# A state-space block: a third state weighed by TensorE, and the second chunk's first in-projection in front of unit 0

## The reference

```python
xz = (hidden_states @ in_proj_w.T).transpose(0, 2, 1)
x, z = jnp.split(xz, 2, axis=1)
# each direction: a convolution of 4 taps over time, a projection to dt, B and C, and then per channel d and state n
def step(h, inp):
    u_t, dt_t, B_t, C_t = inp
    dA = jnp.exp(dt_t[:, :, None] * A)
    h = dA * h + (dt_t * u_t)[:, :, None] * B_t[:, None, :]
    y = jnp.einsum('bdn,bn->bd', h, C_t)
    return (h, y)
y = (y_fwd + y_bwd) * jax.nn.silu(z.transpose(0, 2, 1))
out = y @ out_proj_w.T
```

## Time and profile before

| | us |
|---|---|
| median of 3 runs (lowest, highest) | 8235.12 (8234.53, 8238.75) |
| the profiled execution, its own time | 8231.93 |
| its span in the trace | 8230.1 |
| busy: VectorE, TensorE (matmul), GpSimd, ScalarE | 7156.1, 7136.7, 6715.8, 5349.8 |
| first scan of unit 0 starts at | 728.41 |
| last work of VectorE on unit 255 ends at | about 7181 |

### The profile page before, as it was taken

One profiled execution on the slowest core, in us unless ns is written; L12 is line 12 of the kernel. 1 busy time (PEld: TensorE's weight loads), 2 busy tenths in 40 slices (PEclk: granted clock), 3 DMA queues, 4 the chain that ended last, 5 costly groups with the idle time before them and its releaser, 6 DMA issues. The chain is left out here.

```text
span 8230.1 us, 114768 instructions
## 1 busy us (share of the span) xinstructions
PE 7136.7 (87%) x32512; PEld 4393.1 (53%) x32512; DVE 7156.1 (87%) x7788; ACT 5349.8 (65%) x12640; POOL 6715.8 (82%) x2320
## 2 busy tenths in 40 slices
PE   6578888888888888877899999999999988789999
PEld 3344555555555555554555555555555555534444
DVE  6913999999999999999999999999999999934443
ACT  6634777777777777777777777777777777610000
POOL 5513999999999999999999999999999999821110
PEclk8789999999999999998999999999999999889999
DMA  3363232323232323221323232323233332153442
GB/s 103 90 191 128 70 118 66 118 70 118 67 118 68 119 67 118 68 98 44 113 79 128 76 128 77 131 79 126 89 116 104 104 107 70 63 191 133 136 140 76
DMA packets 557719, 844.05 MB, mean 103 GB/s; under 512 B 129472, under 2 KB 276928, under 8 KB 539712
## 3 DMA queue, kind: packets, MB, share of 16 engines
q1 hardware_dynamic: 557120, 837.10, 31.1%
HBM read 583.89 MB, written 253.02 MB: 102 GB/s over the span
## 5 line engine op out<-in xcount | busy, mean ns | idle before, releaser
L1192 POOL TENSOR_TENSOR scan_w<-scan_du,scan_bcast_b 128x2048 f32<-128x2048 f32 x1023 | 4623.9, 4544 | 45.0 <-DVE scan_h L1239 6.6
L1239 DVE TENSOR_TENSOR_SCAN scan_h<-scan_da,scan_state,scan_w 128x512 f32<-128x512 f32 x2560 | 3185.3, 1276 | 44.2 <-ACT scan_da L1094 27.7
L1094 ACT ACTIVATE scan_da<-scan_delta,scan_prm 128x512 f32<-128x512 f32 x4096 | 2803.1, 685 | 0.0
L973 PE MATMUL scan_yT<-all_ident,scan_hc 128*128 128x128 f32 x10240 | 1540.1, 281 | 660.4 <-DVE scan_hc L1249 659.6
L1239 DVE TENSOR_TENSOR_SCAN scan_hs<-scan_da,scan_state,scan_w 128x512 f32<-128x512 f32 x1536 | 1891.9, 1258 | 45.2 <-ACT scan_da L1094 44.7
L973 PEld LDWEIGHTS scan_yT<-all_ident,scan_hc 128*128 128x128 f32 x10240 | 1175.3, 143 | 1395.5 <-DVE scan_hc L1249 1047.1
L846 PE MATMUL scan_in_ps<-scan_hn,scan_win 128*128 128x512 f32 x3840 | 1732.3, 594 | 13.6 <-issue 13.6
L1249 DVE TENSOR_TENSOR scan_hc<-scan_h,scan_bcast_c 128x512 f32<-128x512 f32 x2560 | 1637.3, 671 | 2.1 <-ACT scan_state L1074 0.7
L1202 POOL TENSOR_TENSOR scan_hp<-scan_hs,scan_bcast_c 128x1024 f32<-128x1024 f32 x512 | 1209.3, 2362 | 49.9 <-DVE scan_hs L1239 42.9
L846 PEld LDWEIGHTS scan_in_ps<-scan_hn,scan_win 128*128 128x128 f32 x3840 | 693.6, 191 | 715.6 <-issue 715.6
L1074 ACT ACTIVATE scan_state<-scan_h 128x1 f32<-128x1 f32 x2560 | 429.5, 168 | 982.8 <-DVE scan_h L1239 977.0
(11 more groups left out here) (122 smaller groups left out, 6918.3 us busy)
## 6 DMA issues: line engine op xcount, KB each, us to landing
yT<-scan_y_out SPq DMA_DIRECT2D x257, 256.0 KB, 2.0
scan_win<-winx SPq DMA_DIRECT2D x128, 512.0 KB, 3.7
xc<-scan_xc_out SPq DMA_DIRECT2D x256, 256.0 KB, 2.0
scan_xc<-xc SPq DMA_DIRECT2D x256, 256.0 KB, 4.1
scan_bcast_b<-bc SPq DMA_DIRECT2D x64, 1024.0 KB, 8.0
scan_bcast_c<-bc SPq DMA_DIRECT2D x64, 1024.0 KB, 8.2
scan_win<-winz SPq DMA_DIRECT2D x128, 512.0 KB, 4.6
scan_x<-x_pad SPq DMA_DIRECT2D x128, 257.5 KB, 2.6
```

What stands on the lines that cost most here:

```text
L973: last = nc.tensor.matmul(yT[:, tb], hc_slot(b, n)[:, tb * P:(tb + 1) * P], ident[:], is_transpose=True, start=(i == 0 and tb == 0), stop= ...
L1094: nc.scalar.activation(da[:, n % 2], delta[:, s], ACT.Exp, scale=decay(b, n)).then_inc(S["exp_done"], 1)
L1192: nc.gpsimd.tensor_tensor(w[:, g], du[:].unsqueeze(1).to_broadcast([P, G, T]), bcast_b[:, g * G:(g + 1) * G], ALU.mult).then_inc(S["w_done ...
L1239: nc.vector.tensor_tensor_scan(flip(b, h_slot(b, n)), flip(b, da[:, n % 2]), flip(b, w[:, n // G, n % G]), state_of(b, n), ALU.mult, ALU.a ...
```

## The change

1. State 1 moves from VN to TN: nine states are weighed by VectorE, three by TensorE (1, 4 and 10). `c_col`, `c_diag` and `hs` grow by one entry each; `y_out` shrinks from two buffers to one, so that `yT_copy(b)` waits until the stores of unit b itself have landed, where it waited for those of unit b - 1.
2. The new state is turned in `dt_ps`, the convolution's bank, in TensorE's step 3, copied in ScalarE's step 7 ahead of the copy out of `in_ps`, and added in TensorE's step 7. The convolution (step 5) now waits for that copy.
3. `C_DIAG_AT` has twelve entries and begins in step 2 (it had eight and began in step 3). `TURN`, the table of units 111 to 127, is gone: they use `NORMAL`.
4. The in-projection of unit 16's x (a = DB) and its copy stand in front of unit 0; the next one (`LATER`) moves to unit 0's steps 0, 2 and 7. SyncE's loads of `hn` and of two blocks of `win` for them move ahead of the last two blocks of `before_scan`.

```diff
-TN = [4, 10]
+TN = [1, 4, 10]
...
-        y_out = sc.sb("y_out", [P, 2, TB, P])
+        y_out = sc.sb("y_out", [P, TB, P])
...
-        EARLY = dict(into=(0, 2), diag=1, copy=5, conv=5, xc=8, proj=8)
-        TURN = dict(diag=1, conv=2, xc=7, proj=8)
-        LATER = dict(into=(8, 10), diag=6, copy=11, conv=11, xc=12, proj=13)
+        EARLY = dict(into=(), diag=1, copy=NS, conv=5, xc=8, proj=8)
+        LATER = dict(into=(0, 2), diag=6, copy=7, conv=9, xc=12, proj=13)
...
-            return [(a, TURN if back(b) and not back(a) else NORMAL)] if a < NU else []
+            return [(a, NORMAL)] if a < NU else []
...
-            if b == 0:
-                return dict(mm=(6, 12), copy=(10, NS - 1), add=(12, NS - 1))
-            return dict(mm=(8, 12), copy=(12, NS - 1), add=(12, NS - 1))
+            return dict(mm=(3, 8, 12), copy=(7, 12, NS - 1), add=(7, 12, NS - 1))
+
+        def turn_bank(k):
+            return in_ps if k else dt_ps
...
-        C_DIAG_AT = (3, 3, 8, 8, 9, 9, 11, 11)
+        C_DIAG_AT = (2, 2, 3, 3, 8, 8, 9, 9, 11, 11, 13, 13)
...
-                for a in range(2):
-                    load_win(DB + a)
...
-                load_hn(1)
...
+                if j == DB // 2 - 1:
+                    hold(sp, S["in_mm"], DB, S["passed"])
+                    load_win(DB)
+                    load_hn(1)
+                    load_win(DB + 1)
...
+                if k == 0:
+                    pe.wait_ge(S["dt_read"], min(b + 2, NU))
+                    pe.wait_ge(S["xc_copied"], min(b + DB + 1, NU) + 2 if b else DB + 2)
...
             def conv_step(a, b):
                 pe.wait_ge(S["dt_read"], min(b + 2, NU))
+                pe.wait_ge(S["h_turn_copied"], b * NTN + 1)
...
             dt_matmul(0)
+            in_step(DB, 0, 0)
+            in_step(DB, 1, 0)
...
-                if b >= 1:
-                    act.wait_ge(S["stored"], stored_to(b - 1))
+                if b >= 0:
+                    act.wait_ge(S["stored"], stored_to(b))
...
+                    if n == turn_steps(b)["copy"][0]:
+                        turn_copy(b, 0)
...
+            act.wait_ge(a_in[DB % 2], (DB // 2 + 1) * (NA * LOAD))
+            in_copy(DB)
             for b in range(NU):
                 unit(b)
```

19 lines of the change are left out of this document (10 added, 9 removed).

## The result

The changed kernel takes 8206.67 us (median of 12 runs, 8201.99 to 8219.13); the kernel before, run beside it, 8234.45 (12 runs, 8222.72 to 8238.75). The ratio is 0.9971 with a 95% interval of 0.9963 to 0.9978: 28 us won. The forecast was 8205, its range 8165 to 8245. The total is right. Of the parts that make it up one has the wrong sign, and another, which was given nothing, cost 5 us. The span of the profiled execution is 8201.3 us.

What follows compares the result with a forecast made beforehand. It took GpSimd's unchanged pitch of 24.86 us as a floor under every unit, beside VectorE's equal pitch. Front -13, steady backward -4, forward -2, units 112 to 127 -8 sum to -27: 8205 us, range 8165 to 8245.

Steps and rivals of the forecast that it cites:

- The front: Up to unit 1: ScalarE's waits for the first two in-projections go; -13 us (-20 to +2).
- Steady backward units: Units 16 to 111: between GpSimd's floor of 2386.6 and VectorE's own 2396 us; -4 us (0 to -9).
- the forecast floor: GpSimd's unchanged pitch of 24.86 us under every unit; 96 x 24.86 = 2386.6 us for units 16 to 111.
- VectorE's own pitch becomes 24.75: Steady units: 24.84 less 0.59 for the removed weighing, plus 0.50 for ScalarE's added copy stalling scan 8.
- TensorE stays off the path as long as its clock holds: Every unit: TensorE gains 0.89 us, 23.2 us a unit backward and 23.7 forward, below 24.84 both times.
- VectorE alone is the bound: Rival: GpSimd's equal pitch is an echo; 152 us over 256 units and 13 at the front, 8067 us; chance 0.05.
- Forward units: Units 128 to 239: clock lapses go, chunk ends cost VectorE 6.2 us each; -2 us (-25 to +40).
- The lapses of the clock: Units 128 to 239: TensorE's clock halves after idle time in one unit of three; worth 21 us, should go.
- The rival's price: Rival of slower chunk ends: 6 us more at each of seven forward ends, 42 us, 8247 us; chance 0.12.
- Units 112 to 127: Units without in-projection, 415.3 us before: -8 us, from -17 at best to +5 if both stalls stay and grow.
- It takes a wait out of ScalarE's tight chain: Units 112 to 127: convolution from step 2 to 5, its copy from 7 to 10; part of the -8 us.
- Chunk ends: Forward ends: columns and y copy wanted sooner, 3 us each, with copy (0.5) and two diagonals (0.6) 4.1 more.

Runs made afterwards that it cites:

- the front alone: Kernel before plus only the early first in-projection, its loads and copy in front of unit 0, two turned states and two y buffers kept: 8217.73 us, ratio 0.9985.
- the filler: Changed kernel plus TensorE matmuls whose result nobody reads, two groups in units 111 to 127 and one in units 240 to 255: 8175.64 us, ratio 0.9926.

## Why the prediction came out, and where it didn't

*The total*: 8205 forecast, 8206.67 measured. -13, -4, -8, -2 and 0 met -16 (with -3 in the rest of chunk 0), -8, +10, -10 and +5, and -6 from a stretch in which nothing changed. Some of that is luck.

*The front*: right in mechanism, -16 for -13. I had put 4 us on hn's load going ahead of the last stores and the first scan at 737; it started at 732.96 in the profiled run. In other kernels with the same front it started at 731 to 748 us, so single executions differ here by as much as the term itself. Alone it was worth 14 us.

*Steady backward units*: 2387.3, within 0.7 us of the forecast floor of 2386.6, yet not because of the floor. The step that failed is the sentence that VectorE may be shortened and GpSimd's unit is still the pitch. With GpSimd 1.1 us a unit lighter nothing moved. "VectorE's own pitch becomes 24.75" was 24.70, with 0.35 of stall where I had 0.5; that the scan which stalls is scan 8, behind ScalarE's copy, is as in the trace. By the prediction's own sum VectorE needed 2396, and -4 was a choice between that and the floor; the 0.05 us a unit and six chunk ends at 2.7 us each, where I had 3.4, are the whole distance to 2387.3. That the result lies on the floor is luck. What I had not seen is the second way to the same scan: "TensorE stays off the path as long as its clock holds" was argued from its busy time, 23.2 of 24.84 us. In the changed kernel the turn in step 3 hangs behind 9.7 us of TensorE's work, and that ring closes in 24.68 us. The rival "VectorE alone is the bound" (8067) is refuted too: the stall in front of scan 8 doesn't go with GpSimd.

*Forward units*: -10.4 for -2, inside its range, by two sizes. The lapses of the clock went, as forecast (granted clock 1.00), and chunk ends cost VectorE 2807.1 - 112 x 24.70 = 40.7 us, 5.8 each, where I had 6.2. The pitch made the rest: 24.70 and not 24.75 gives 5.6 us. But the seven are not alike. Chunk 8 begins behind a backward end and takes 397.9, 2.7 us over its sixteen pitches; the six behind it take 401.5 on average, 6.3 over. So a forward end does cost over 6 us, which the prediction had named as a sign of being wrong although its own term was 6.2, and the sum came out because one of the seven was cheap. The rival's price, 6 us more an end than I took, did not come.

*Units 112 to 127*: the failed step. The prediction took -8 here, and +10.1 came. "It takes a wait out of ScalarE's tight chain" is wrong, since the copy in step 10 has its own successor, exponential 11, and behind 3 us of idle time twice the convolution runs at 1.2 GHz for most of its time. I had read the clock of 0.89 in the earlier trace rows and the idle time, and treated both as given; in the kernel before the convolution stood between the two idle stretches, after the change both stand ahead of it, with 1.1 us of work between them. I had allowed +5 at most. Nor is the move the whole of it: with the convolution in step 2 two turned states took 416.3 us (the front alone) and three took 436.8. So the third state, with what goes with it, cost 20 us in the old place and 9 in the new one, a term that the prediction put at nothing because it went by the floor. The filler, which changes nothing but TensorE's idle time and with it the clock, takes all of it away and 18 us more.

*The last chunk*: I gave it no term because it sat on GpSimd's floor. It has the same illness, milder: the granted clock is 0.95, two of three units take about 25.2 us instead of 24.70, and that is +5, gone with the filler.

*Chunk ends*: the waits for columns (2.75 us) and the later stores are as forecast, and for the reason given. Before the change the last column landed 5.0 us after the first scan of unit 144 and was wanted 4.5 after it; now it lands 4.8 after it (4339.40 + 12.95) and is wanted 2.1 after it. The third load moved nothing there (below); the diagonals are asked for 2.4 us sooner, where I had 1.8.
